# Row normalisation in a fused three-pass attention kernel: the subtract-and-scale step moved from VectorE to ScalarE, and every engine's order laid out anew

## The chip, the cores and the metric

The kernel runs on one core of a Trainium2 chip. The metric is the device time of one launch in microseconds. Engines are named as in the profile: PE (TensorE; PEld is its weight load), DVE (VectorE), ACT (ScalarE), POOL (GpSimd), SP (SyncE, here only an issuer of DMAs).

## The reference

A batch of 32 elements (`x`: 256 rows of 256, `ctx`: 120 rows of 256) goes through four transformer-like layers. Cut to what matters:

```python
def _ln(x, g, b):                       # in every layer, after every residual sum
    mu = mean(x, -1); var = mean((x - mu)**2, -1)
    return (x - mu) * rsqrt(var + EPS) * g + b
# L0: x += attn(ln(x)) causal, 16 heads; x += xattn(ln(x), ctx); x += gelu(ln(x) @ W_fc) @ W_mproj
# L1: x = ln(x + attn(x) masked); x = ln(x + xattn(x, ctx)); x = ln(x + relu(x @ W1) @ W2)
# L2: x = ln(x + xattn(x, ctx) masked)
# L3: x = ln(x + xattn(x, ctx) with 16 heads of 64)
```

All is float32, each layer has its own weights, and the softmaxes subtract the row maximum.

## The kernel before

The program makes three **passes** over the 32 elements: `l0` is layer L0, `l1` layer L1, `l2` layers L2 and L3 together. Between passes an element's rows go through DRAM (`between`). Within a pass an element is cut into **steps** with names such as `stats.1.0` or `scores_max.own.3`: `own` and `other` are the first and second attention, `ff` the feed-forward part, `three` the attention of L3, and 0 to 3 number the places where rows are normalised or turned.

**The order is written out by hand.** `LISTS[pass][engine]` gives every step a time in units of one element's period; `Step` adds `START[pass]` and the element's number, and `run` sorts each engine's steps by that sum (L367 and on). So each engine works on about six elements at once, always in the same cyclic order. An engine never looks past its next instruction: if that one waits on a semaphore, all behind it wait. The numbers decide the order only; nothing waits for a clock. The eight PSUM banks are handed out in the order of PE's list, each to the bank whose reader is listed to finish first, so a PE group can also wait for the DVE or ACT step that empties its bank.

**One normalisation** (key `0` to `3`) runs over these steps, each tile holding 2 x 128 rows:

- DVE `stats`: two `bn_stats`, two `bn_aggr` (L1023 to L1031) give `meanvar`.
- POOL `stats`: `veps` = variance + eps (L633), `rstd` = `veps` to the power -0.5 (L639).
- DVE `norm`: two `tensor_scalar`, one for each 128 rows, `xh` = (x - mean) * rstd (L1043, the loop of `kind == "norm"`).
- PE `norm`: four transposes of `xh` into a bank (L1328); ACT `norm`: gain and shift on the way out of the bank into `ht` and `ht_hi` (L757); POOL `ht_lo` where a product is split in parts.
- In `l1` and `l2` POOL `xb` makes `xh` * gain + shift as the next residual (L676, L681).

Normalisations 0, 1, 2 are made in `l0`, 1, 2, 3 in `l1`, 1 and 3 in `l2`: 8 for each element, 256 in all, of which 6 for each element feed PE; number 3 ends a pass and feeds only `xb` and the store.

**Around it.** Of an attention's `q` and `k`, three bfloat16 parts are made by ACT, DVE (`split_rest`, L1082), ACT and POOL, spilled to DRAM and loaded back stacked (`qstack`, `kstack`; SP, L558 and L572). `scores_max` is a first product on PE whose row maxima DVE takes (L1111, L1115); `scores_exp` the second, masked by DVE in `l1` (L1130) or on POOL in `l0` (L701), exponentiated by ACT (L879); `probs_v` the product with `v_aug`, which DVE writes (L1095); `project_out` ends it and DVE adds the residual into `xn` (L1210). SP loads `x_in` (L530) two elements ahead at most, after DVE's `project_out.own` of the element two before has read the buffer, and `ct` (L539) after PE's last `project_k3` of the element two before (in `l2`).

## Time and profile before

| what | value |
|---|---|
| median of 3 runs | 4299.66 us (4295.97 to 4301.73) |
| the profiled execution | 4300.15 us, its span 4298.4 us |
| PE busy, DVE busy | 4069.6 us (95%), 3742.6 us (87%) |
| ACT busy, POOL busy | 2718.3 us (63%), 1863.6 us (43%) |
| mean granted PE clock | 0.980 of full |
| DMA moved | 512.52 MB, 119 GB/s |
| PE idle in the span | 4298.4 - 4069.6 = 228.8 us |

Busy times overlap across engines. The passes have different loads, so the shares of the whole span are averages over three machines that differ; the rows below take them apart.

### The profile page before, as it was taken

Reading aid. Unit: us, or ns where it says so; the run is one execution under the profiler, and the core shown is the slowest. Engines: PE = TensorE matmul, PEld = TensorE weight load, DVE = VectorE, ACT = ScalarE, POOL = GpSimd, SP = SyncE. Lnnn points to the kernel's source line nnn. Section 1 sums busy time; section 2 is a strip of 40 time slices with the busy share of each in tenths; the row PEclk is TensorE's granted clock in tenths of the full one; section 3 lists DMA queues with packets and bytes.
Section 4 is the critical chain, followed back from the end, with each engine's and each line's share of the span. In section 5 each row is a group of like instructions: output and inputs, shape, how many; then the busy total and the mean of one; then the engine's idle time right before and its main releaser. Section 6 shows DMA issues by size and latency. Waiting matters only on the chain. (4 is left out here: it accounts for less than half of the span.)

```text
span 4298.4 us, 106109 instructions
## 1 busy us (share of the span) xinstructions
PE 4069.6 (95%) x36480; PEld 3458.8 (80%) x36480; DVE 3742.6 (87%) x12517; ACT 2718.3 (63%) x7085; POOL 1863.6 (43%) x3089
## 2 busy tenths in 40 slices
PE   4899999999999899999999999998999999999998
PEld 3688888888887678778778888777888888888887
DVE  4899999999998799999999999986888888888886
ACT  2566666667676555555555555554777777777776
POOL 4455545455554234445445455445222232222333
PEclk8999999999999899999999999999999999999999
DMA  4554545454554454544544544534223222222220
GB/s 149 151 153 142 156 142 161 137 155 140 149 152 117 127 169 117 147 138 119 146 139 125 158 125 133 152 109 119 81 61 84 69 75 75 70 82 71 75 72 27
DMA packets 403752, 512.52 MB, mean 119 GB/s; under 512 B 133648, under 2 KB 371216, under 8 KB 381712
## 3 DMA queue, kind: packets, MB, share of 16 engines
q1 hardware_dynamic: 395824, 495.51, 40.1%
q10 hardware_dynamic: 7392, 10.24, 0.7%
q8 instruction: 291, 4.77, 0.5%
q14 instruction: 245, 2.01, 0.2%
HBM read 266.30 MB, written 236.72 MB: 117 GB/s over the span
## 5 line engine op out<-in xcount | busy, mean ns | idle before, releaser
L879 ACT ACTIVATE probs_own<-bank 128x384 f32<-128x384 f32 (+2 forms) x1280 | 648.6, 564 | 286.1 <-DVE bank L1130 250.8
L633 POOL TENSOR_SCALAR veps<-meanvar 128x2 f32<-128x2 f32 x256 | 71.6, 280 | 1015.6 <-DVE meanvar L1031 1013.1
L1263 PE MATMUL bank<-w_ff,ffh 128*128 128x256 f32 x2048 | 490.1, 385 | 1.0
L1263 PE MATMUL bank<-kstack_own,qstack_own 96*128 96x256 bf16 (+2 forms) x3072 | 355.4, 250 | 102.9 <-issue 54.2
L1111 DVE CUSTOM_DVE_ANT_0 bank<-bank,mask_words 128x256 f32<-128x256 f32 x1024 | 398.3, 455 | 50.5 <-PE bank L1263 50.3
L1111 DVE DVE_READ_ACCUMULATOR2_ANT nmf_own<- 128x1 f32 x3072 | 429.1, 140 | 0.0
L1263 PEld LDWEIGHTS bank<-w_ff,ffh 128*128 128x128 f32 x2048 | 372.2, 190 | 65.5 <-issue 14.0
L879 ACT ACTIVATE probs_other<-bank 120x512 f32<-120x512 f32 x512 | 289.6, 603 | 161.3 <-PE bank L1263 161.1
L676 POOL TENSOR_TENSOR xb<-xh,vectors_l 128x256 f32<-128x256 f32 x320 | 229.8, 740 | 344.7 <-DMA out<-xb 202.8
L1263 PEld LDWEIGHTS bank<-kstack_own,qstack_own 96*128 96x128 bf16 x3072 | 242.7, 99 | 166.9 <-issue 95.3
L944 ACT ACTIVATE probs_other<-bank,negmax 128x120 f32<-128x120 f32 x1024 | 355.8, 380 | 31.0 <-DVE negmax L1229 31.0
L1111 DVE CUSTOM_DVE_ANT_0 bank<-bank,causal_rows 128x128 f32<-128x128 f32 (+1 forms) x1024 | 328.0, 391 | 23.0 <-PE bank L1263 22.7
L1263 PE MATMUL bank<-qstack_own,kstack_own 98*128 98x256 bf16 (+2 forms) x2560 | 320.8, 264 | 12.0 <-DMA qstack_own<-nm_t_own 9.2
L1130 DVE TENSOR_TENSOR bank<-bank,mask_words 128x512 f32<-128x512 f32 x512 | 319.1, 685 | 2.5 <-PE bank L1263 2.5
L1115 DVE TENSOR_REDUCE nmf_other<-bank 128x4 f32<-128x480 f32 x512 | 305.2, 646 | 14.7 <-PE bank L1263 14.6
L1263 PE MATMUL bank<-ht_hi,w_ff_hi 128*128 128x256 f32 x1024 | 314.2, 307 | 1.5 <-DVE nmf_own L1111 0.2
L1263 PE MATMUL bank<-probs_own,v_aug_own 128*32 128x256 f32 (+2 forms) x5120 | 299.6, 369 | 14.7 <-POOL probs_own L701 12.8
L1263 PE MATMUL bank<-ht_lo,w_ff_hi 128*128 128x256 f32 x1024 | 291.5, 285 | 0.0
L1263 PE MATMUL bank<-ht_hi,w_ff_lo 128*128 128x256 f32 x1024 | 291.0, 284 | 0.0
L1263 PEld LDWEIGHTS bank<-qstack_own,kstack_own 98*128 98x128 bf16 (+1 forms) x2560 | 231.7, 105 | 72.4 <-issue 15.0
L1111 DVE CUSTOM_DVE_ANT_0 bank<-bank,m_rows 128x120 f32<-128x120 f32 x1024 | 253.1, 316 | 28.5 <-PE bank L1263 28.5
L730 POOL TENSOR_TENSOR ht_lo<-ht,ht_hi 128x256 fp32r<-128x256 f32 x192 | 146.8, 786 | 245.0 <-ACT ht L757 245.0
(200 smaller groups left out, 12668.0 us busy)
## 6 DMA issues: line engine op xcount, KB each, us to landing
qstack_own<-q_parts SPq DMA_DIRECT2D x96, 768.0 KB, 5.7
kstack_own<-k_parts SPq DMA_DIRECT2D x64, 768.0 KB, 6.4
qstack_other<-q_parts SPq DMA_DIRECT2D x64, 768.0 KB, 6.1
q_parts<-q_parts_own SPq DMA_DIRECT2D x96, 384.0 KB, 3.5
k_parts<-k_parts_own SPq DMA_DIRECT2D x64, 384.0 KB, 2.5
q_parts<-q_parts_own SPq DMA_DIRECT2D x96, 256.0 KB, 3.0
q_parts<-other_parts SPq DMA_DIRECT2D x64, 384.0 KB, 3.0
other_words<-k_parts SPq DMA_DIRECT2D x64, 360.0 KB, 3.6
```

What stands on the lines that cost most here:

```text
L633: nc.gpsimd.tensor_scalar(veps[key][:, :], meanvar[key][:, :, 1], r["norms"][key]["eps"], None, ALU.add).then_inc(veps_ready.sem, 1)
L676: ins = nc.gpsimd.tensor_tensor(xb[key][:, t, :], xh[src][:, t, :], mul, ALU.mult)
L730: ins = nc.gpsimd.tensor_tensor(ht_lo[key][:, f, :], ht[key][:, f, :], ht_hi[key][:, f, :].bitcast(F32), ALU.subtract)
L879: nc.scalar.activation(probs[key][0:rows, j % a.slots, 0:n], bank_of(u)[0:rows, 0:n], ACT.Exp, scale=a.scale).then_inc(a_done.sem, 1)
L944: ins = nc.scalar.activation(probs3[:, j % 4, n, :], bank[:, n * S2:(n + 1) * S2], ACT.Exp, scale=-1.0, bias=negmax3[:, j, n:n + 1], accum ...
L1111: ins = v.tensor_tensor_reduce(scores, scores, add, -1.0, LIMIT if a.masked == "each" else 3.0e38, ALU.add, ALU.min, nmf[key][:, t, at:at ...
L1115: ins = v.tensor_reduce(nmf[key][:, t, first:first + FT * len(heads) - FT + 1:FT], bank[:, 0:len(heads) * nk].rearrange("p (h k) -> p h k" ...
L1130: v.tensor_tensor(p, p, add, ALU.add).then_inc(masked_by_dve.sem, 1)
L1263: return nc.tensor.matmul(out, lhsT, rhs, start=first, stop=True, skip_group_check=True)
```

## The change

The subtract-and-scale step leaves DVE. ACT makes `xh` as one `activation` of type Identity for each 128 rows, scale * x + shift, with a scale and a shift for each row: the scale is `rstd`, the shift is -mean * rstd. POOL makes the shift in two new instructions of 2 values for each partition: minus the mean (L640 in the new file), then times `rstd` (L649). The new step is named `xhat`; `xhat_ready` now counts ACT's steps, so everything that waited for DVE's `norm` (PE's transposes, POOL's `xb`, the writers of `xn`) waits for ACT. DVE's `bn_aggr` gets one more wait (`minus_ready`), and two mask steps of `l2` get waits on steps of their own engine. All numbers in `LISTS` and `START` are new.

```diff
-    xhat_ready = counts("xhat_ready", "DVE", ("norm",))
+    xhat_ready = counts("xhat_ready", "ACT", ("xhat",))
...
                 nc.gpsimd.tensor_scalar(veps[key][:, :], meanvar[key][:, :, 1], r["norms"][key]["eps"], None,
                                         ALU.add).then_inc(veps_ready.sem, 1)
...
+                nc.gpsimd.tensor_scalar(shift_of[key][:, :], meanvar[key][:, :, 0], -1.0, None, ALU.mult).then_inc(minus_ready.sem, 1)
...
-                nc.gpsimd.tensor_tensor(rstd[key][:, :], veps[key][:, :], half[:, :], ALU.pow).then_inc(rstd_ready.sem, 1)
+                nc.gpsimd.tensor_tensor(rstd[key][:, :], veps[key][:, :], half[:, :], ALU.pow).then_inc(pow_ready.sem, 1)
+                if w.new(minus_ready, u.tag):
+                    g.wait_ge(minus_ready.sem, w.value(minus_ready, u.tag))
+                settle(g)
+                if w.new(pow_ready, u.tag):
+                    g.wait_ge(pow_ready.sem, w.value(pow_ready, u.tag))
+                nc.gpsimd.tensor_tensor(shift_of[key][:, :], shift_of[key][:, :], rstd[key][:, :], ALU.mult).then_inc(rstd_ready.sem, 1)
...
+            elif kind == "xhat":
+                src = r["norms"][key]["src"]
+                x = x_in[:, u.element % 2] if src == "x_in" else xn[src]
+                if w.new(rstd_ready, ("stats", key, 0)):
+                    act_e.wait_ge(rstd_ready.sem, w.value(rstd_ready, ("stats", key, 0)))
...
+                for t in range(QT):
+                    ins = affine(xh[key][:, t, :], x[:, t, :], rstd[key][:, t:t + 1], shift_of[key][:, t:t + 1])
+                ins.then_inc(xhat_ready.sem, 1)
...
-                for t in range(QT):
-                    ins = v.tensor_scalar(xh[key][:, t, :], x[:, t, :], meanvar[key][:, t, 0:1], rstd[key][:, t:t + 1],
-                                          ALU.subtract, ALU.mult)
-                ins.then_inc(xhat_ready.sem, 1)
...
-START = {"l0": 0.00000, "l1": 32.78129, "l2": 66.17862}
+START = {"l0": 0.00000, "l1": 32.60944, "l2": 66.29325}
```

**Place 1, SP in `l1`,** up to the loads of `qstack_own` and `kstack_own` for the next element (L572 before, L575 with the change; `k_parts<-k_parts_own` is the spill of the third part of `k`, and in brackets stand the semaphores waited for). Before:

```order
L572 DMA other_words<-k_parts 96x1920 [waits a_full,spilled_k0_other,spilled_k1_other,spilled_k2_other]
L572 DMA qstack_other<-q_parts 96x4096 [waits spilled_q0_other,spilled_q1_other,spilled_q2_other]
L584 DMA between_2<-xb 128x2x256 [waits xb_ready]
L539 DMA ct<-in_ctx 128x2x120 [waits d_full]
L558 DMA k_parts<-k_parts_own 128x512
L530 DMA x_in<-between_1 128x2x256 [waits xb_ready,stored]
L572 DMA qstack_own<-q_parts 96x4096 [waits a_full,spilled_q0_own,spilled_q1_own,spilled_q2_own]
L572 DMA kstack_own<-k_parts 96x4096 [waits spilled_k0_own,spilled_k1_own,spilled_k2_own]
```

With the change:

```order
L533 DMA x_in<-between_1 128x2x256 [waits xb_ready,stored]
L575 DMA other_words<-k_parts 96x1920 [waits a_full,spilled_k0_other,spilled_k1_other,spilled_k2_other]
L561 DMA q_parts<-q_parts_own 128x512
L575 DMA qstack_other<-q_parts 96x4096 [waits spilled_q0_other,spilled_q1_other,spilled_q2_other]
L561 DMA k_parts<-k_parts_own 128x512 [waits lo_ready]
L575 DMA qstack_own<-q_parts 96x4096 [waits a_full,spilled_q0_own,spilled_q1_own,spilled_q2_own]
L575 DMA kstack_own<-k_parts 96x4096 [waits spilled_k0_own,spilled_k1_own,spilled_k2_own]
L587 DMA between_2<-xb 128x2x256
```

The store (`between_2<-xb`) and the load of `ct` stood ahead of the third spill of `k`; the store is now behind both stack loads and `ct` further up. From the row of negated maxima of `own` (`nm_rows.own`, L577), which waits for the end of `scores_max.own`, to that spill there were 13 other issues and are now 10.

**Place 2, PE in `l1`,** the end of the work that lies between the last `scores_exp.own` of one element (`qstack_own,kstack_own`, which frees both stacks) and the first `scores_max.own` of the next (`kstack_own,qstack_own`, which reads them anew). Ahead of these rows stood, after the last `scores_exp.own`, the 12 products of `project_q.other`. Before:

```order
L1263 MATMUL bank<-other_words,qstack_other 128x120 x16
L1263 MATMUL bank<-ct,w_other 128x120 x4
L1328 MATMUL bank<-ident,x_in 128x128 x4
L1263 MATMUL bank<-other_words,qstack_other 128x120 x8
L1263 MATMUL bank<-probs_own,v_aug_own 32x256 x8
L1328 MATMUL bank<-ident,xh 128x128 x4
L1263 MATMUL bank<-other_words,qstack_other 128x120 x8
L1263 MATMUL bank<-probs_own,v_aug_own 32x256 x8
L1263 MATMUL bank<-kstack_own,qstack_own 128x256 x8
L1263 MATMUL bank<-own_hi 128x256
```

With the change (ahead of these rows: 4 of `w_ff,ffh`, 20 of `other_words,qstack_other` and the same 12):

```order
L1288 MATMUL bank<-other_words,qstack_other 128x120 x8
L1353 MATMUL bank<-ident,x_in 128x128 x4
L1288 MATMUL bank<-ct,w_other 128x120 x4
L1353 MATMUL bank<-ident,xh 128x128 x4
L1288 MATMUL bank<-other_words,qstack_other 128x120 x4
L1288 MATMUL bank<-w_other,ct 120x256 x2
L1288 MATMUL bank<-kstack_own,qstack_own 128x256 x4
L1288 MATMUL bank<-probs_own,v_aug_own 32x256 x16
L1476 MATMUL bank<-identb,nm_parts_other 96x128 x2
```

The two groups of 8 `probs_own,v_aug_own` are moved behind the first `scores_max`; 4 `w_ff,ffh` and the 2 of `w_other,ct` are moved in. The trace counts each such float32 product twice (x8 for 4 rows here), and a product of `kstack`, `qstack` or `own_hi` once.

**Place 3, PE in `l2`,** ahead of the transposes of a freshly loaded `x_in`, which SP may load only after `project_out.own` (`w_own,ctx_t_own`) of the element two before and the DVE step behind it. With the change the whole stretch is:

```order
L1288 MATMUL bank<-w_own,ctx_t_own 128x256 x4
L1599 MATMUL bank<-ident,probs_other 120x128 x4
L1288 MATMUL bank<-kstack_own,qstack_own 128x120 x4
L1288 MATMUL bank<-w_own,ct 120x256 x2
L1288 MATMUL bank<-kstack_own,qstack_own 128x120 x4
L1288 MATMUL bank<-ct,ff_xu 128x120 x8
L1288 MATMUL bank<-kstack_own,qstack_own 128x120 x8
L1288 MATMUL bank<-ct,ff_xu 128x120 x8
L1353 MATMUL bank<-ident,x_in 128x128 x4
```

Before, only this was left of a longer one, in which a mask product, 16 of `vectors,probs_other`, 8 transposes of `probs_other` and 36 of `w_fc` stood between `w_own,ctx_t_own` and the first row here (the third row is the same transposes of `x_in`):

```order
L1263 MATMUL bank<-w_fc_hi,ot_lo 128x256
L1263 MATMUL bank<-kstack_own,qstack_own 128x120 x12
L1263 MATMUL bank<-ct,ff_xu 128x120 x8
L1263 MATMUL bank<-w_own,ct 120x256 x2
L1263 MATMUL bank<-kstack_own,qstack_own 128x120 x4
L1328 MATMUL bank<-ident,x_in 128x128 x4
L1574 MATMUL bank<-ident,probs_other 120x128 x4
L1263 MATMUL bank<-kstack_own,qstack_own 128x120 x4
L1263 MATMUL bank<-ct,ff_xu 128x120 x8
```

## Rows read from the trace of the kernel before

**Rows 1.** Windows: columns us, then busy (xcount) of PE, PEld, DVE, ACT, POOL; clock; DMA
```profile
306.10:1270.30 964.20, 937.88 (x8653) 792.76 (x8653) 899.60 (x2994) 653.17 (x1520) 511.26 (x920) 1.00 0.51 148
1715.90:2672.50 956.60, 912.30 (x7899) 762.49 (x7898) 902.00 (x2817) 524.02 (x1094) 472.86 (x756) 0.98 0.47 136
3200.00:4100.00 900.00, 900.00 (x8423) 797.45 (x8422) 747.77 (x2777) 677.00 (x2240) 261.53 (x409) 1.00 0.26 73
```

**Rows 2.** Source L1043, l0 and l1: ns min/median/max, first and last start
```profile
L1043 DVE TENSOR_SCALAR xh<-x_in,meanvar,rstd x48: 397/405/412, 306.1 to 1270.3; 128x256 f32<-128x256 f32 x48
...
L1043 DVE TENSOR_SCALAR xh<-xn_own,meanvar,rstd x44: 403/407/410, 1715.9 to 2672.5; 128x256 f32<-128x256 f32 x44
```

**Rows 3.** Waits of PE in those stretches (us, times, longest): l0, then l1
```profile
PE bank L1263 <- DMA qstack_own<-q_parts: 19.3, 22, 1.7
...
PE bank L1263 <- issue: 39.9, 21, 3.5
```

**Rows 4.** Timeline of PE in l1: start, us, what
```profile
1972.98 1.03 PE L1263 MATMUL bank<-kstack_own,qstack_own 96*128 96x256 bf16 x8 [1.89 <-issue]
...
2000.73 1.89 PE L1263 MATMUL bank<-w_ff,ffh 128*128 128x256 f32 x8
...
2007.47 1.03 PE L1263 MATMUL bank<-w_other,ct 128*120 128x256 f32 x4
...
2008.34 0.38 PE L1263 MATMUL bank<-qstack_own,kstack_own 98*128 98x256 bf16 x2
...
2014.75 1.07 PE L1263 MATMUL bank<-probs_own,v_aug_own 128*32 128x256 f32 x16
...
2018.06 1.03 PE L1263 MATMUL bank<-kstack_own,qstack_own 96*128 96x256 bf16 x8 [2.24 <-issue]
```

**Rows 5.** Timeline of SP's DMA issues in l1
```profile
1959.02 0.53 SPq L558 DMA_DIRECT2D k_parts<-k_parts_own  x1
...
1965.20 0.32 SPq L572 DMA_DIRECT2D kstack_own<-k_parts  x1
...
2009.03 0.32 SPq L572 DMA_DIRECT2D qstack_own<-q_parts  x1
```

**Rows 6.** Source L558, the spill issued at 1959.02
```profile
DMA to landing us min/median/max: 6.1/6.1/6.1
```

**Rows 7.** Source L572, the load issued at 1965.20
```profile
DMA to landing us min/median/max: 7.7/7.7/7.7
```

**Rows 8.** Timeline of DVE in l1
```profile
1972.32 0.71 DVE L1095 TENSOR_TENSOR v_aug_own<-bank,vectors_l 128x256 f32<-128x256 f32 x2
```

**Rows 9.** Lines, DVE, the stretch of l1: busy us, mean ns
```profile
L1043 DVE TENSOR_SCALAR xh<-xn_ff,meanvar,rstd 128x256 f32<-128x256 f32 x42 | 21.2, 547 | 0.1
...
L1043 DVE TENSOR_SCALAR xh<-xn_own,meanvar,rstd 128x256 f32<-128x256 f32 x43 | 15.8, 407 | 0.0
...
L1043 DVE TENSOR_SCALAR xh<-xn_other,meanvar,rstd 128x256 f32<-128x256 f32 x42 | 15.3, 405 | 0.0
```

**Rows 10.** Lines, ACT, the stretch of l1
```profile
L757 ACT ACTIVATE ht<-bank,columns_l 128x256 f32<-128x256 f32 x84 | 42.8, 563 | 19.1 <-PE bank L1328 19.1
```

**Rows 11.** Lines, POOL, the stretch of l0
```profile
L639 POOL TENSOR_TENSOR rstd<-veps,half 128x2 f32<-128x2 f32 x69 | 59.6, 864 | 10.9 <-POOL veps L633 10.4 <-DVE ot_raw_own L1165 0.4
...
L633 POOL TENSOR_SCALAR veps<-meanvar 128x2 f32<-128x2 f32 x69 | 21.4, 310 | 158.2 <-DVE meanvar L1031 158.2
```

**Rows 12.** Timeline of PE in l2
```profile
3505.80 2.00 PE L1263 MATMUL bank<-ct,ff_xu 128*128 128x120 f32 x16
...
3533.47 1.89 PE L1263 MATMUL bank<-w_own,ctx_t_own 128*128 128x256 f32 x8
```

**Rows 13.** Timeline of SP in l2
```profile
3536.60 0.38 SPq L530 DMA_DIRECT2D x_in<-between  x1
```

**Rows 14.** Source L530, loads of x_in in l2
```profile
DMA to landing us min/median/max: 2.6/2.7/4.8
```

More of the change, by code:

```diff
@@ new lines @@
+            scores_exp.own.9/1.95966 scores_exp.own.14/1.96311 scores_exp.own.12/1.96721 probs_v.own.2/2.01105
+            probs_v.own.3/2.02801 project_out.own.0/2.14529 norm.1.0/2.33009 project_q.other.0/2.39363 project_v.other.0/2.69626
+            scores_max.other.0/2.81664 scores_max.other.5/2.82192 scores_max.other.3/2.87023 scores_max.other.4/2.88377
+            scores_max.other.2/2.88906 scores_max.other.7/2.89434 scores_max.other.1/2.90378 scores_max.other.6/2.95438
+            negate_t.other.0/3.12816 scores_exp.other.7/3.24469 scores_exp.other.5/3.25017 scores_exp.other.1/3.25566
@@ new lines @@
+            scores_exp.own.4/2.04528 scores_exp.own.12/2.09166 scores_exp.own.11/2.09686 scores_exp.own.8/2.10205
+            scores_exp.own.14/2.10725 probs_v.own.0/2.11476 probs_v.own.1/2.13594 scores_exp.own.13/2.15942
+            scores_exp.own.9/2.20585 scores_exp.own.15/2.21105 project_k.other.0/2.33823 probs_v.own.2/2.40926
+            probs_v.own.3/2.43044 project_out.own.0/2.60333 norm.1.0/2.79363 project_q.other.0/2.83751 scores_max.other.5/3.25742
+            scores_max.other.1/3.26243 scores_max.other.2/3.26744 scores_max.other.3/3.27244 scores_max.other.4/3.27745
@@ L195 @@
+            spill_q.other.1/2.95410 spill_q.other.2/2.98879 stack_k.other.0/3.01121 stack_q.other.0/3.05317
+            nm_rows.other.0/3.48139 store.x.0/7.24343
         """,
@@ L445, in run @@
     veps_ready = counts("veps_ready", "POOL", ("stats",))
+    minus_ready = counts("minus_ready", "POOL", ("stats",))
+    pow_ready = counts("pow_ready", "POOL", ("stats",))
     rstd_ready = counts("rstd_ready", "POOL", ("stats",))
@@ L1056, in _ @@
                         dve.wait_ge(d_full.sem, w.value(d_full, tag, 1))
+                else:
+                    tag = latest(w, d_done, "scores_max", "own", len(r["atts"]["own"].max_jobs()), 1)
+                    if u.element % NB and w.new(d_done, tag, 1):
+                        settle(dve)
+                        dve.wait_ge(d_done.sem, w.value(d_done, tag, 1))
                 v.tensor_scalar(m_rows[:, :, :], m_in[:, :, :], 0.0, -BIG, ALU.not_equal, ALU.mult).then_inc(mask_ready.sem, 1)
@@ L1064, in _ @@
                         dve.wait_ge(a_full.sem, w.value(a_full, tag, 1))
+                else:
+                    tag = latest(w, masked_by_dve, "mask_scores", "own", r["atts"]["own"].exp_count(), 1)
+                    if u.element % NB and w.new(masked_by_dve, tag, 1):
+                        settle(dve)
+                        dve.wait_ge(masked_by_dve.sem, w.value(masked_by_dve, tag, 1))
                 rows = bank_of(u)[0:S2, 0:T // 2].bitcast(BF16)
```

354 lines of the change are left out of this document (173 added, 181 removed).

## The prediction

> **What bounds the kernel now.** I first cut the trace into one steady stretch for each pass [rows 1]; the reader should look at PE's busy time against the stretch, then at DVE's, then at the clock. The first starts of a repeated instruction give the period of an element [rows 2]: 24 pairs of `x_in` in `l0` are 23 periods, (1270.3 - 306.1) / 23 = 41.9 us, and 22 pairs of `xn_own` in `l1` are 21, (2672.5 - 1715.9) / 21 = 45.55 us. For one element that makes:
>
> - `l0`: PE busy 937.88 / 23 = 40.8 us, idle 1.1; DVE 39.1 us (93%).
> - `l1`: PE busy 912.30 / 21 = 43.4 us, idle 2.1; DVE 42.95 us (94%); clock 0.98.
> - `l2`: PE busy the whole 900 us; DVE 83%, ACT 75%. PE is the bound, nothing of another engine shows.
>
> So what can be won by moving work between the other engines lies in `l0` and `l1`. The clock of 0.98 in `l1` means 4% of the time at 1.2 instead of 2.4 GHz, which is 0.02 x 45.55 = 0.9 us of work lost for each element; in `l0` and `l2` it is 1.00. PE's own floor in `l1` is thus 43.4 - 0.9 = 42.5 us.
>
> Next I asked what PE waits for. In `l0` it is `qstack_own`, 19.3 / 23 = 0.84 us for each element; in `l1` 39.9 / 21 = 1.90 us, put down to "issue", so to nothing the view could name [rows 3]. With DVE at 94% one would guess DVE. The rows say otherwise: the gap ends at the first `scores_max.own` [rows 4], which waits for a bank and for the two stacks. The third part of `k` was spilled at 1959.02, landed 6.1 later, at 1965.1; `kstack_own` was issued at 1965.20 and landed 7.7 later, at 1972.9 [rows 5 to 7]. PE went on at 1972.98 [rows 4], while DVE was still writing `v_aug_own` until 1973.03 [rows 8]. **The gap of `l1` is the DMA chain spill, stack, product, not DVE**; DVE's idle 2.6 us are mostly PE's gap passed on.
>
> Two things hold that chain back. The spill is issued late, at the end of a burst of SP's issues. And the stacks can't be loaded before the last `scores_exp.own` of the element before has read them: it starts at 2008.34, `qstack_own` is issued at 2009.03, PE's other work lasts until 2014.75 + 1.07 = 2015.8, and the product starts at 2018.06 [rows 4, 5].
>
> **What the change removes from DVE.** In `l1` 21.2 + 15.8 + 15.3 = 52.3 us over 21 elements, 2.5 us each [rows 9]; DVE goes from 42.95 to 40.5 us. In `l0` it is as much or a little more, in `l2` two thirds. Since DVE isn't what PE waits for, this alone is worth nothing at once; it is room. Without it a gapless `l1` of 43 us would hold DVE at 100%, with it at 93%, a share that `l0` has now [rows 1].
>
> **What ACT gets.** Two instructions with a scale and a shift for each row. The nearest row is L757, the same kind with the same operands, from a bank: 0.563 us [rows 10]; a pair is 1.13 us at most, 3.4 us for an element with three. ACT was busy 653.17 / 23 = 28.4 us in `l0`, 25.0 us in `l1` [rows 1], so it ends at 31.8 of 42 and 28.4 of 45. In `l2`, 75% of 41.4 us (31.1) grows by 2.3 to 81%. I cost this at nothing; what hides it is that idle time, and if ACT's queue is late at that place, it comes out as the second rival.
>
> **What POOL gets.** Minus the mean is L633's kind, 0.31 us; the product with `rstd` is not in the trace: between L633's 0.31 and L639's 0.86, which is a power of the same two values [rows 11]. I take 0.4, nearer the former, for it has no power. Together 0.7 us, 2.1 for an element, on an engine busy 22.2 of 41.9 us in `l0`: nothing. As latency it counts: the chain from statistics to `xh` grows by 0.7 us on POOL (0.6 to 1.2) and by 1.13 - 0.8 = 0.3 us on ACT, so 1.0 us (0.9 to 1.5). It shows bare where no other element's work covers it: at the first element and at the last row sum of the program, 2 us in all. The new waits (`minus_ready`, the two mask steps) name work that was issued long before on engines which are in order anyway: nothing.
>
> **What the new orders do, `l1`.** Place 1: between the row of maxima and the third spill of `k` there are three issues fewer (the store among them, which also no longer moves its bytes beside the spill). An issue takes 0.3 to 0.5 us [rows 5], with the gaps between them about 0.5, so the spill goes out some 1.5 us earlier. Place 2: PE's cover was 7.5 us (2008.34 to 2015.8). The two groups of `probs_own` leave it (1.0 us each, of 1.07 with the tail), four `w_ff` (1.75, of 1.89) and the two `w_other,ct` (0.87, from 2007.47 to 2008.34) come in [rows 4]: 8.1 us. The stacks need, from the last `scores_exp.own`, 0.7 to the issue of `qstack_own`, 0.4 for the next issue, about 7.5 to land, 0.1 to start: 8.7 us. So the gap can't fall under 0.6 us and is 0.8 if the spill is a little late still, against 1.90: **1.1 us**. The clock fell in the gaps; at less than half their length I count a third of its 0.9 us as won back: **0.3 us**. Some 31 elements of `l1`: 31 x 1.4 = 43 us. The bounds: nothing (both are eaten by a longer landing), and 31 x 2.8 = 87 us.
>
> **`l0`.** The wait there is the same chain for `q`. Its rows around the stacks hardly move, except that the store now goes out just ahead of `qstack_own` instead of just behind. I take nothing; the bounds are 31 x 0.84 = 26 us gained and, for one issue of 0.4 us more, 12 lost.
>
> **`l2`.** PE is full, so nothing is to be won, but place 3 takes cover from the load of `x_in`. Before, the load was issued 3536.60 - 3533.47 = 3.1 us after `project_out.own` began and landed after 2.7 (at most 4.8) [rows 12 to 14]: it needs 5.8 us, at worst 7.9. The new stretch has 1.75 for `project_out`, twice 1.85 for `ct,ff_xu` (2.00 with the tail) [rows 12], 0.87 for `w_own,ct`, and 1.3 for 20 short products: 7.6 us. It holds by 1.8 us; at the worst landing it would be 0.3 us late. I take nothing; the bound is 31 x 0.3 = 9 us lost.
>
> **Sum.** -43 + 0 + 0 + 2 = -41 us. The profiled execution took 4300.15 us, so 4259 us; the median of the runs, 4299.66, is 0.5 us lower, which changes nothing.
>
> **The rivals.**
>
> *The gaps close fully.* If the spill is early and the stacks land fast beside less traffic, `l1` gives 31 x 2.8 = 87 and `l0` 20: 4300 - 107 + 2 = 4195 us. For it: DVE now has the room. Against: cover of 8.1 us for 8.7.
>
> *The normalisation chain comes onto PE's path (slower).* In none of the stretches did PE's transposes wait for `xh`; what it waited for is the row of each stretch shown [rows 3]. The chain grows by 1.0 us, and six normalisations for each element of the three passes feed PE: 192 chains. From 0.21 us shown of each, the 41 us are gone; with 0.4 us it is 77 - 41 = 36 us slower: 4336 us. For it: ACT serves `xh` in order among exponentials, which themselves wait for DVE's masks. Against: the orders were laid out with the longer chain in them.
> The length of POOL's instructions speaks for it too: `rstd` of 256 values in all takes 0.86 us on average in `l0` and 0.31 `veps` [rows 11], more than such small work asks. The Trainium skill's page "SBUF — State Buffer", section "Who interferes with whom", says that VectorE instructions with two inputs in SBUF and GpSimd's reads lock each other out for a whole instruction. By that rule each of the now four small instructions can be held up by such a DVE step, where it was two; the chain would grow by up to twice a DVE step more, and the rival gets likelier.
>
> *The moved work only changes the place of the wait.* A new order finds another late step, in `l0` and `l1`, and gives back what place 1 and 2 bring: 4298 us. If only the longer cover of place 2 holds (0.6 us for each of 31 elements), it is 4300 - 19 + 2 = 4283 us.
>
> **How the numbers follow.** Forecast 0.50; gaps closed 0.15; only place 2, 0.07; wait moved, no change, 0.09; chain on PE's path or another loss 0.19. A measurement here tells 0.2% (8.6 us) from no change. Faster by more: 0.50 + 0.15 + 0.07, less 0.02 for their weak ends, 0.70; same 0.09 and 0.01 of these, 0.10; slower 0.19 and 0.01, 0.20. The likeliest time is 4259 us. The range goes from the closed gaps (4195, and 5 us for the rest) to the price of the chain at 0.4 us: 4190 to 4336 us.
>
> **What would show it.** Right: in `l1` PE's longest wait drops under 1 us for each element, the period to about 44.2 us, the clock to 0.99, `kstack_own` issued within 0.5 us of `qstack_own`; DVE's busy time in `l1` near 40.5 us for each element; ACT's `xh` at 0.5 to 0.6 us; `l2` still full. Wrong: waits of PE for ACT's `xh` or for a bank read by DVE, PE idle in `l2`, or a spill of `k` that still lands 6 us before its stack is issued late.

## The result and the profile after

| | before | after |
|---|---|---|
| median of 4 runs, us | 4299.64 (4295.97 to 4301.73) | 4236.94 (4230.44 to 4241.72) |
| ratio | 1 | 0.9858, 95% interval 0.9846 to 0.987 |
| span of the profiled execution, us | 4298.4 | 4228.7 |
| PE busy, DVE busy, us | 4069.6, 3742.6 | 4036.3, 3593.2 |
| ACT busy, POOL busy, us | 2718.3, 1863.6 | 2976.9, 1990.4 |
| mean granted PE clock | 0.980 | 0.988 |

The time fell by 62.7 us; 41 were forecast. The two profiled spans, which the rows below take apart, differ by 69.7 us, for the profiled execution of after is the fastest of its four (4230.44 us). The sum is near, its parts are not.

I cut the spans at SP's loads of `x_in`, one for each element and pass: the 17th and 32nd lie in the steady part of `l0`, the 43rd and 64th in that of `l1`, the 73rd and 96th in that of `l2`. SP timeline of after, columns start and us:

```profile
646.86 0.38 SPq L533 DMA_DIRECT2D x_in<-in_x  x1
...
1263.03 0.38 SPq L533 DMA_DIRECT2D x_in<-in_x  x1
...
1777.25 1.73 SPq L533 DMA_DIRECT2D x_in<-between  x1
...
2691.21 0.36 SPq L533 DMA_DIRECT2D x_in<-between  x1
...
3131.12 0.38 SPq L533 DMA_DIRECT2D x_in<-between  x1
...
4095.15 0.38 SPq L533 DMA_DIRECT2D x_in<-between  x1
```

Each distance by its count of elements is a period: (1263.03 - 646.86) / 15 = 41.08 us. With the same loads of before (660.13, 1287.97, 1823.01, 2778.31, 3205.00 and 4157.37):

| stretch | before, us | after, us | difference |
|---|---|---|---|
| start to load 17 | 660.1 | 646.9 | -13.3 |
| loads 17 to 32: period of `l0` | 41.86 | 41.08 | -11.7 in all |
| loads 32 to 43, `l0` into `l1` | 535.0 | 514.2 | -20.8 |
| loads 43 to 64: period of `l1` | 45.49 | 43.52 | -41.3 in all |
| loads 64 to 73, `l1` into `l2` | 426.7 | 439.9 | +13.2 |
| loads 73 to 96: period of `l2` | 41.41 | 41.91 | +11.7 in all |
| load 96 to the end | 141.0 | 133.5 | -7.5 |

So up to load 32 (`l0`) 25 us were won, on the way to the 64th (mostly `l1`) 62, then 25 were lost in the turn to `l2` and in `l2`, and 7 came back at the end. In the turn from `l0` to `l1` (loads 32 to 43) the clock was 0.952 and is 0.977, and PE's busy time fell from 490.5 to 471.6 us; by 0.048 x 535.0 - 0.023 x 514.2, up to 14 of the 20.8 us can be the clock. The steady windows of after, same columns as [rows 1], in the order `l0`, `l1`, `l2`:

```profile
646.90:1263.00 616.10, 607.49 (x5642) 518.51 (x5640) 569.97 (x1861) 473.70 (x1080) 350.90 (x691) 1.00 0.53 151
1777.20:2691.20 914.00, 887.45 (x7898) 745.05 (x7897) 846.70 (x2689) 598.67 (x1219) 491.25 (x884) 1.00 0.50 143
3131.12:4095.15 964.03, 964.03 (x8926) 847.21 (x8925) 773.81 (x2832) 747.95 (x2462) 327.25 (x530) 1.00 0.26 73
```

The same loads 43 to 64 of before:

```profile
1823.00:2778.30 955.30, 910.38 (x7904) 760.83 (x7896) 901.56 (x2815) 523.75 (x1092) 472.87 (x756) 0.99 0.47 136
```

For one element, `l1` before (the same 21 elements): PE busy 43.35, idle 2.14 us; after: 887.45 / 21 = 42.26 busy, 1.26 idle, DVE 846.70 / 21 = 40.3 us. PE in `l2` is as full as it was, and yet an element takes 0.50 us longer with the same number of products (8926 against 8928 over 23 elements). What is left of [rows 3] in `l1` is one wait at the same place:

```profile
PE bank L1288 <- issue: 26.5, 21, 1.7
```

PE and SP around it, to be laid beside [rows 4, 5], and the landings of the two loads, beside [rows 6, 7]:

```profile
1960.03 0.60 PE L1288 MATMUL bank<-qstack_own,kstack_own 98*128 98x256 bf16 x4
...
1967.14 1.08 PE L1288 MATMUL bank<-w_other,ct 128*120 128x256 f32 x4
...
1969.20 0.60 PE L1288 MATMUL bank<-kstack_own,qstack_own 96*128 96x256 bf16 x4 [0.97 <-issue]
```

```profile
1956.02 0.36 SPq L561 DMA_DIRECT2D k_parts<-k_parts_own  x1
...
1960.95 0.32 SPq L575 DMA_DIRECT2D qstack_own<-q_parts  x1
...
1961.52 0.32 SPq L575 DMA_DIRECT2D kstack_own<-k_parts  x1
```

```profile
DMA to landing us min/median/max: 5.3/5.3/5.3
...
DMA to landing us min/median/max: 7.6/7.6/7.6
```

The third part of `k` is spilled 5.5 us before `kstack_own` is issued and lands at 1961.3, `kstack_own` goes out 0.57 us behind `qstack_own` (0.91 before), lands 7.6 us later, at 1969.1, and PE starts at 1969.20. The chain stands as the prediction described it. From the last `scores_exp.own` (1960.03) PE has work until 1968.2; the product starts 9.2 us after it.

In `l0` PE's wait for `qstack_own`, which the prediction took as staying, nearly went. Before and after, over 15 elements:

```profile
PE bank L1263 <- DMA qstack_own<-q_parts: 11.8, 14, 1.4
...
PE bank L1288 <- DMA qstack_own<-q_parts: 2.4, 6, 0.5
```

### The profile page after: what moved, and what is told of

Same layout as the page of the kernel before. It is cut to its first block and busy times, and to the rows that moved or that the text cites. A ratio compares the mean times of both kernels' runs of the same rounds, so it can differ in the third digit from the quotient of the medians.

```text
span 4228.7 us, 106986 instructions
## 1 busy us (share of the span) xinstructions
PE 4036.3 (95%) x36480; PEld 3441.3 (81%) x36480; DVE 3593.2 (85%) x12005; ACT 2976.9 (70%) x7597; POOL 1990.4 (47%) x3601
## 5 line engine op out<-in xcount | busy, mean ns | idle before, releaser
L905 ACT ACTIVATE probs_own<-bank 128x384 f32<-128x384 f32 (+2 forms) x1280 | 674.5, 563 | 173.2 <-PE bank L1288 106.1
L1288 PE MATMUL bank<-kstack_own,qstack_own 96*128 96x256 bf16 (+2 forms) x3072 | 384.7, 247 | 66.3 <-issue 40.3
L1288 PE MATMUL bank<-qstack_own,kstack_own 98*128 98x256 bf16 (+2 forms) x2560 | 339.5, 263 | 7.0 <-DMA qstack_own<-nm_t_own 2.9
L1136 DVE CUSTOM_DVE_ANT_0 bank<-bank,causal_rows 128x256 f32<-128x256 f32 (+1 forms) x1024 | 330.0, 392 | 18.5 <-PE bank L1288 17.0
L723 POOL TENSOR_TENSOR other_parts<-remains_other,other_parts 128x120 bf16<-128x120 f32 (+1 forms) x256 | 147.2, 596 | 385.5 <-issue 377.2
L1288 PE MATMUL bank<-probs_own,v_aug_own 128*32 128x256 f32 (+2 forms) x5120 | 287.8, 365 | 9.2 <-POOL probs_own L711 8.0
```

What stands on the lines that cost most here:

```text
L723: ins = nc.gpsimd.tensor_tensor(f3[2][:, f, :], x32[:, f, :], f3[1][:, f, :], ALU.subtract)
L905: nc.scalar.activation(probs[key][0:rows, j % a.slots, 0:n], bank_of(u)[0:rows, 0:n], ACT.Exp, scale=a.scale).then_inc(a_done.sem, 1)
L1136: ins = v.tensor_tensor_reduce(scores, scores, add, -1.0, LIMIT if a.masked == "each" else 3.0e38, ALU.add, ALU.min, nmf[key][:, t, at:at ...
L1288: return nc.tensor.matmul(out, lhsT, rhs, start=first, stop=True, skip_group_check=True)
```

## The experiments

Line numbers in rows of an experiment are those of its own file. Everything measured, the kernels before and after on top; the ratio is to runs of before made beside each kernel (their medians lie between 4297.20 and 4303.49 us), and the periods are read from the same loads of `x_in` in one execution each. Where a kernel has the tables and the code of before in a pass, its period there shows what one reading is worth: 41.86 to 42.03 us in `l0`, 45.49 and 45.23 in `l1`, 41.41 in all for `l2`. A difference under 0.3 us in `l1` or 0.2 in `l0` is therefore not told.

| kernel | median, us | ratio to before (95%) | `l0` | `l1` | `l2` |
|---|---|---|---|---|---|
| before | 4299.64 | | 41.86 | 45.49 | 41.41 |
| after | 4236.94 | 0.9846 to 0.9870 | 41.08 | 43.52 | 41.91 |
| op_only | 4314.93 | 1.0019 to 1.0042 | 42.52 | 45.07 | 41.41 |
| order_only | 4303.55 | 0.9998 to 1.0016 | 42.33 | 44.43 | 41.89 |
| dve_load | 4271.77 | 0.9925 to 0.9950 | 41.52 | 43.97 | 41.90 |
| sp_l1 | 4284.98 | 0.9943 to 0.9968 | 41.96 | 44.76 | 41.41 |
| pe_l1 | 4248.62 | 0.9862 to 0.9889 | 41.96 | 43.71 | 41.41 |
| both_moves | 4247.95 | 0.9857 to 0.9890 | 41.98 | 43.39 | 41.41 |
| cover_l1 | 4232.89 | 0.9824 to 0.9851 | 41.00 | 43.43 | 41.94 |
| best_b | 4223.99 | 0.9799 to 0.9830 | 41.10 | 43.34 | 41.41 |
| l2_old | 4231.53 | 0.9825 to 0.9852 | 41.11 | 43.57 | 41.41 |
| cover_l2_old | 4223.16 | 0.9803 to 0.9830 | 41.10 | 43.40 | 41.41 |
| split_l2 | 4330.82 | 1.0055 to 1.0081 | 42.03 | 45.23 | 42.17 |
| best_a | 4238.26 | 0.9849 to 0.9879 | 41.05 | 43.41 | 41.63 |

### The operation alone, and the order alone

```diff
 op_only: tables of before, code of after
-   "DVE": ... norm.1.0/2.29221 ...
+   "ACT": ... xhat.1.0/2.29221 ...
 order_only: tables of after, code of before
-   "ACT": ... xhat.1.0/2.29018 ...
+   "DVE": ... norm.1.0/2.29018 ...
```

One of eight such steps is shown for each. order_only keeps the two waits of the mask steps that the change added.

> The order tables and START of the kernel before; only xh is moved to ACT (each DVE norm step becomes an ACT step with the same number). Theory A (the gain is in PE's stretches and comes from the order: the DMA chain of l1 and what PE has ahead of it): PE still waits about 1.9 us for each element of l1, and the time stays within 9 us of before, 4291 to 4309 us. Theory B (DVE's relief of 2.5 us for each element is what pays): l1's period falls from 45.5 us towards 43.5 and l0's from 41.9 towards 41.1, so 4300 - 31 x 2.8 = 4213 to 4260 us. Theory C (the longer chain to xh comes onto PE's path, hidden in after by its order): slower than 4309 us.

> The order tables and START of the changed kernel, with xh still made by DVE (each ACT xhat step becomes a DVE norm step with the same number, POOL makes no shift). Theory A: l1's period 43.5 us, l0's 41.1, l2's 41.9 as in after; 4237 to 4250 us. Theory B: DVE at 87.6/22-like 42.8 us of 43.5 is too full, PE waits for banks that DVE reads, l1's period stays above 44.5 us: 4270 us or more.

Measured: 4314.93 and 4303.55 us. Neither half gives anything: the operation alone loses 14 us (against the 4300.76 us of before beside it), the order alone changes nothing that can be told, and together they win 63. PE's waits say why. op_only, `l1` over 21 elements, then `l0` over 15 (us, times, longest):

```profile
PE bank L1270 <- issue: 23.1, 21, 1.7
...
PE bank L1335 <- ACT ht L746: 17.4, 21, 0.9
...
PE bank L1270 <- DMA qstack_own<-q_parts: 17.6, 15, 1.7
...
PE bank L1270 <- DVE remains_own L1089: 10.0, 15, 1.0
```

In `l1` the gap of the DMA chain is smaller but there, and PE now waits 0.83 us for each element for ACT's `ht`, that is for an ACT queue made longer without being laid out for it (the reason is argued; that it is new is shown). `l1` is even so not longer than before (45.07 us, 0.42 less than that reading); what makes the kernel slower is `l0`, 0.66 us longer, where PE waits for the stack and for DVE. The wait for ACT is the second rival of the prediction, alive in the old order. order_only, `l1` and `l0`:

```profile
PE bank L1256 <- DVE nmf_other L1108: 16.9, 21, 1.4
...
PE bank L1321 <- DVE xh L1026: 9.2, 21, 0.4
...
PE bank L1256 <- DVE nmf_own L1104: 6.8, 15, 0.5
...
PE bank L1321 <- DVE xh L1026: 5.8, 14, 0.7
```

Of the DMA gap in `l1` 4.1 us are left (14 times, 0.6 at the longest), 0.9 in `l0`, and PE waits for DVE, for the row maxima and for `xh`: (16.9 + 9.2) / 21 = 1.24 us for each element of `l1`. Theory A as I had put it (the order does it all) falls, and so does B (the relief does it all), though B's account of this kernel, DVE too full for the new order, fits what PE waits for; C holds for op_only.

### Is it DVE's time, or `xh` that comes late?

```diff
 dve_load: after, with "norm" steps put back into DVE's tables at the numbers of ACT's xhat
+            elif kind == "norm":
+                ...
+                    for n in range(3):
+                        ins = v.bn_stats(junk[:, junks % 2 * 3 + n, :], ident[:, :])
```

> The changed kernel, with three small BN_STATS of a constant (128 x 128, their result is not used) put on DVE wherever order_only has DVE's norm step; xh stays on ACT. In order_only PE waited in l1 for DVE's nmf_other (16.9 us) and for DVE's xh (9.2 us) over 21 elements, in after for neither. Theory L (DVE's time at that place is what the new order needs free): l1's period rises from 43.5 towards 44.4 us, l0's from 41.1 towards 42.3, the wait for nmf_other is back, 4237 + up to 60 = 4270 to 4300 us. Theory M (not the load, but that xh itself comes late behind DVE's queue): the wait for nmf_other stays away, l1's period 43.5 to 43.8 us, 4237 to 4248 us.

Measured: 4271.77 us, 35 of the 63 us are lost again. PE's waits in `l1`, and the added work (41.4 us in 20.7 elements, 2.0 us each, against the 2.5 us that left DVE):

```profile
PE bank L1281 <- issue: 15.8, 21, 1.1
...
PE bank L1281 <- DVE nmf_own L1129: 5.5, 21, 0.5
...
PE bank L1281 <- DVE nmf_other L1133: 4.7, 21, 0.2
...
L1052 DVE BATCH_NORM_STATS2 junk<-ident 128x6 f32<-128x128 f32 x186 | 41.4, 278 | 0.0
```

The waits for the maxima are back, though not as long as in order_only, and the period rises by 0.45 us in `l1` and 0.44 in `l0`. So DVE's time counts in the new order (theory L), for about half of the difference to order_only in `l1` and a third in `l0`. Some of the rest may be load too, for DVE's busy time rises by only 1.7 us for each element of `l1` (40.3 to 42.0), in order_only by 2.4. The one wait of `l1` that order_only has and this kernel has not is the one for DVE's `xh`: there the transposes of `xh` start 45 ns behind DVE's semaphore in all 21 elements, 0.6 us later than their usual pace. That this wait makes up the rest is argued, not shown.

### The DMA chain of `l1`, on the kernel before

```diff
 sp_l1, table of SP in l1          pe_l1, table of PE in l1
-   spill_k.own.2/0.98890          -   project_q.own.0/0.33548
+   spill_k.own.2/0.93400          +   project_q.own.0/0.30500
-   store.x.0/6.96671
+   store.x.0/7.16550
```

> The kernel before with two steps of SP's table of l1 moved: the third spill of k goes right behind the second (about 2.2 us earlier, its data is there), the store behind kstack_own's load. In the trace of before, kstack_own is issued 0.9 us behind qstack_own (1965.20 against 1964.29) and lands 7.7 us later. Theory A1 (the late spill is half of l1's gap): kstack_own goes out 0.4 to 0.5 us behind qstack_own, the gap of 1.90 us shrinks by 0.5 (up to 0.9 if the store no longer slows the landing), and part of the 0.9 us of clock comes back: 31 x 0.7 = 22 us, 4278 us (4262 to 4285). Its rival (the spill is hidden behind the last scores_exp.own anyway and the landing stretches): 4300 us.

> The kernel before with one step of PE's table of l1 moved: project_q.own (12 products, 1.4 us) goes ahead of the first scores_max.own, so that PE has 1.4 us more to do while the stacks land. Theory A2 (PE's cover against the landing sets the gap): the gap falls from 1.90 to about 0.5 us, the clock rises from 0.98, l1's period from 45.5 to about 43.5 us; 31 x 1.9 = 59 us, 4241 us (4225 to 4260). Its rival (DVE at 94% holds l1: a bank isn't free, or scores_max is read later): the gap comes back at another place, 4290 us or more.

Measured: 4284.98 us, `l1` 0.73 us shorter (0.7 expected), and 4248.62 us, `l1` 1.78 us shorter (1.9 expected). PE's wait over 21 elements, of sp_l1 and of pe_l1, and the latter's window (columns as in [rows 1]):

```profile
PE bank L1246 <- issue: 33.7, 21, 2.2
```

```profile
PE bank L1246 <- issue: 10.0, 16, 2.0
...
1815.80:2733.70 917.90, 904.35 (x7908) 752.16 (x7903) 897.76 (x2815) 522.77 (x1092) 472.54 (x756) 1.00 0.49 142
```

Before it was 40.5 us in the same 21 elements; the clock of pe_l1 is 1.00. One step of PE moved by 0.03 of an element makes the time 1.25% shorter, some 54 us, with nothing else touched: the gap of `l1` was the DMA chain, and PE's cover is what it is measured against. DVE is busy 897.76 of 917.9 us here, 98%: a full DVE did not keep the gap open. Both together:

> The kernel before with the moves of sp_l1 and pe_l1 together, xh on DVE, l0 and l2 untouched. Alone they gave l1 periods of 44.76 and 43.71 us against 45.49. In pe_l1 DVE is busy 897.76 of 917.9 us, 42.75 us for each element. Theory V (with the gap closed DVE's 42.75 us hold l1, and that is what the move of xh to ACT takes away): l1's period falls by no more than 0.2 us to 43.5 to 43.7 us, 4240 to 4249 us. Its rival (the two add up: the DMA chain still sets l1): 43.71 - 0.73 = 42.98 us, DVE at 99%, 4249 - 22 = 4227 us.

Measured: 4247.95 us, `l1` 43.39 us. The window of both_moves:

```profile
1815.80:2720.00 904.20, 896.35 (x7856) 744.34 (x7855) 888.87 (x2802) 519.36 (x1086) 469.37 (x752) 1.00 0.51 142
```

DVE is at 98.3%, and PE itself at 99.1%. The second move brings 0.32 us where it had brought 0.73 alone, and in the median nothing that can be told from pe_l1: the two moves don't add up, as theory V has it, and `l1` stops at some 43.4 us. But PE's busy time is 43.0 us of them and DVE's 42.7, so this run does not show that it is DVE that stops it. That the moved `xh` opens room is shown by dve_load and order_only, in the new order.

### More cover in the changed kernel

```diff
 cover_l1: after, table of PE in l1        best_b: cover_l2_old, table of DVE in l1
-   probs_v.own.2/2.40926                  -   negate.other.1/3.43366
+   probs_v.own.2/2.39500                  +   negate.other.1/3.41500
-   probs_v.own.3/2.43044
+   probs_v.own.3/2.39600
```

> The changed kernel with two steps of PE's table of l1 moved: probs_v.own 2 and 3 (32 products, 1.87 us) go ahead of the first scores_max.own, which waits for kstack_own. PE's gap there is 1.27 us for each element. Theory A2: cover of 8.15 + 1.87 = 10.0 us against the 9.2 us that the stacks need from the last scores_exp.own: the gap closes, l1's period falls from 43.5 to 42.3 us, 31 x 1.25 = 39 us, 4198 us. Its rival (probs_own is not yet there so early, or DVE reads scores_max later and becomes the bound): the wait moves, 4230 us or more.

Measured: 4232.89 us, `l1` 43.43 us instead of 42.3; the interval overlaps that of after. The wait only moved, as the rival said. PE and DVE of cover_l1 in one element:

```profile
2018.85 0.60 PE L1270 MATMUL bank<-kstack_own,qstack_own 96*128 96x256 bf16 x4 [0.45 <-issue]
...
2020.33 0.28 PE L1458 MATMUL bank<-identb,nm_parts_other 128*96 128x128 bf16 x2 [0.88 <-DVE nm_parts_other L1151]
```

```profile
2016.91 0.17 DVE L1147 CAST nm_parts_other<-nmf_other 128x32 bf16<-128x32 f32 x1
...
2019.27 0.43 DVE L1118 CUSTOM_DVE_ANT_0 bank<-bank,mask_words 128x256 f32<-128x256 f32 x1 [2.18 <-PE bank L1270]
...
2020.00 0.18 DVE L1151 TENSOR_TENSOR nm_parts_other<-nmf_other,nm_parts_other 128x32 bf16<-128x32 f32 x1
```

PE's next wait is for `nm_parts_other`. DVE had nothing to do from 2017.1 to 2019.27, but that short step stands in its list behind a `scores_max.own` that waits for PE. So I moved it ahead:

> cover_l2_old with one further edit, in DVE's table of l1: negate.other.1 goes ahead of scores_max.own.8. In cover_l1 PE waits at negate_t.other 0.88 us for nm_parts_other, which DVE writes only behind the first scores_max.own, though DVE is idle for 2.2 us just before it. Theory Q (PE waits for what is queued behind a waiting step of DVE): the wait is gone, l1's period falls from 43.4 to 42.6 us (42.2 at best), 31 x 0.85 = 26 us, 4223 - 26 = 4197 us. Its rival (the stacks' load holds l1 at 43.4 us whatever else is moved): the time stays at 4223 us and the wait shows at the first scores_max.own.

Measured: 4223.99 us against 4223.16 of cover_l2_old, `l1` 43.34 us. The wait for `nm_parts_other` is gone (it does not appear in PE's waits any more) and nothing is won: PE waits for the next steps of DVE instead, in part in pieces that the view of waits counts as busy. PE of best_b around the place, and DVE:

```profile
2018.04 0.60 PE L1270 MATMUL bank<-kstack_own,qstack_own 96*128 96x256 bf16 x4
2018.92 0.36 PE L1270 MATMUL bank<-own_hi 128*128 128x256 f32 x1 [0.29 <-DVE nmf_own L1118]
...
2028.13 0.39 PE L1270 MATMUL bank<-ht_hi,w_ff_hi 128*128 128x256 f32 x1
```

```profile
2027.40 0.67 DVE L1217 TENSOR_TENSOR xn_own<-bank,xb 128x512 f32<-128x512 f32 x1
```

Four products of `scores_max.own` hold PE for 0.36 us when nothing stops them (timeline of cover_l1, 2020.45 to 2020.81); here they take 0.88 us, of which 0.29 are shown as a wait for DVE's row maxima (6.0 us in the 21 elements). The product at 2028.13 starts 0.06 us behind the end of DVE's `xn_own`, 0.39 us after the one ahead of it where 0.11 is the pace, and a third place loses 0.11 us behind `nmf_own`. The three make 0.9 us, what the wait for `nm_parts_other` was. From 2017.90 to 2028.8 the view shows no gap of DVE, so in this stretch PE follows DVE, though DVE is at 93% over the whole element. Whether a better order of that stretch would shorten `l1` was not tried.

### `l2`: a full PE whose period depends on the order

```diff
 l2_old: after, all tables of l2 from before (norm.k on DVE as xhat.k on ACT)
 cover_l2_old: l2_old and cover_l1 together
 split_l2: before, table of PE in l2
-   scores_max.own.5/1.16617 scores_max.own.3/1.32809 turn3.three.6/3.48900
+   scores_max.own.5/1.21600 scores_max.own.3/1.34400 turn3.three.6/3.49950
-   turn3.three.5/3.56846 scores_exp.own.0/1.61386 scores_exp.own.6/1.67545
+   turn3.three.5/3.61360 scores_exp.own.0/1.57750 scores_exp.own.6/1.70450
```

> The changed kernel with only the tables of l2 taken from before (DVE's norm steps as ACT's xhat steps at the same numbers). In both kernels PE is never idle in l2, yet its period is 41.41 us before and 41.91 after; PE goes 37 times for each element from one kind of product to another before, 43 times after. Theory S (each such change costs PE about 0.50 / 6 = 0.083 us): the period is 41.41 us again, 31 x 0.50 = 15 us are won, 4221 us. Theory X (the 0.50 us come with xh on ACT and the longer chain): the period stays at 41.9 us and the time at 4237 us.

> The kernel before with six steps of PE's table of l2 moved by 0.2 to 1.9 us each, so that PE goes 44 instead of 37 times for each element from one kind of product to another; nothing is added, and no other table changes. Theory S (a change costs 0.083 us): l2's period 41.41 + 7 x 0.083 = 41.99 us with PE still never idle, 31 x 0.58 = 18 us slower, 4318 us. Its rival (PE's time is the sum of its products in any order): 41.41 us, 4300 us. If PE shows idle time in l2, the moves made a wait and the run tells less.

> The changed kernel with the two moves of cover_l1 and the tables of l2 of before. If both theories hold and the two don't touch each other: 4237 - 39 - 15 = 4183 us. If l1's gap doesn't close by the moves: 4221 us.

Measured: l2_old has its period of 41.41 us again, with `xh` on ACT; order_only has 41.89 with `xh` on DVE, op_only 41.41 with `xh` on ACT. In all kernels the old tables of `l2` give 41.41 and the new ones 41.9 us, wherever `xh` is made; theory X is out. The time falls less than its 15 us, to 4231.53, and the interval overlaps that of after: the old tables take 142.6 us from load 96 to the end where the new ones take 133.5. split_l2 has 42.17 us, 0.76 more for 7 more changes of product, where 0.58 were expected. 0.06 of it are idle time of PE and 0.22 a wait that the busy share hides: the last `qstack_own,kstack_own` ahead of `w_v_hi,ct_parts` takes 0.33 us instead of 0.11 in all 23 elements, and the next product starts 44 ns behind the semaphore of ACT's `probs_other`. So 0.48 us are left for the 7 changes. l2_old together with cover_l1 is 4223.16 us, 14 us better than after: the two intervals don't meet. So far theory S held. Its test in the other direction:

```diff
 best_a: cover_l2_old, table of PE in l1 and in l2
-   negate_t.other.0/3.45392
+   negate_t.other.0/3.46500
-   scores_max.own.2/1.23870 scores_max.own.7/1.39392 scores_exp.own.5/1.67191 scores_exp.own.6/1.67545
+   scores_max.own.2/1.26350 scores_max.own.7/1.32900 scores_exp.own.5/1.63250 scores_exp.own.6/1.63300
-   scores3.three.2/2.80064 scores3.three.3/2.80064 turn3.three.3/3.07137
+   scores3.three.2/2.73150 scores3.three.3/2.73160 turn3.three.3/3.02450
```

> cover_l2_old with two further edits of PE's tables. In l1 negate_t.other, for which PE waited 18.6 us over 21 elements in cover_l1, goes 0.5 us later, behind two scores_max.own. In l2 seven steps are moved so that PE goes 31 instead of 37 times for each element from one kind of product to another. By theory S with 0.083 to 0.109 us for each change (l2_old and split_l2) l2's period falls from 41.41 to 40.76 to 40.91 us, 31 x 0.5 to 0.65 = 16 to 20 us; rival: the steps that are moved ahead wait for their data and the period stays. In l1 the wait of 0.9 us shrinks to 0.2 us: 31 x 0.7 = 22 us. Sum: 4223 - 18 - 22 = 4183 us; with neither 4223 us.

Measured: 4238.26 us; `l2` has 31 changes of product for each element and 41.63 us, more than the 41.41 with 37. (The edit in `l1` halved PE's wait there, from 18.6 to 9.4 us, and its period stayed at 43.41 us.) The window of `l2` over 23 elements still shows PE as never idle:

```profile
3127.50:4085.10 957.60, 957.60 (x8929) 840.38 (x8928) 771.45 (x2830) 755.28 (x2463) 295.96 (x529) 1.00 0.26 74
```

The rival that had been named is at work in it, unseen: one product of `probs_own,v_aug_own` and the last `qstack_own,kstack_own` ahead of `w_v_hi,ct_parts` take 0.13 and 0.12 us more than their pace in all 23 elements, and what follows each starts 44 ns behind a semaphore, of DVE's `ot_lo` and of ACT's `probs_own`. Without these waits it would be 41.38 us, and theory S wanted 40.76 to 40.91. **The price per change falls** all the same.

What does set it can be read one pair at a time, as the distance from one group's start to the next one's. The same eight products of `ct,w_own`, in before and in after:

```profile
3639.52 1.10 PE L1263 MATMUL bank<-ct,w_own 128*128 128x120 f32 x8
3640.39 0.36 PE L1263 MATMUL bank<-ht_hi,w_q_hi 128*128 128x256 f32 x1
3640.59 0.28 PE L1263 MATMUL bank<-ht_lo,w_q_hi 128*128 128x256 f32 x1
```

```profile
3558.44 1.10 PE L1288 MATMUL bank<-ct,w_own 128*128 128x120 f32 x8
3559.47 0.87 PE L1288 MATMUL bank<-ffh,other_parts 120*64 120x256 f32 x6
```

3640.39 - 3639.52 = 0.87 us when products of 128*128 weights follow, 3559.47 - 3558.44 = 1.03 us when those of 120*64 follow. About half of the 0.16 us is only counted at another product: in before the first `ht_hi,w_q_hi` has 0.20 us to the next one (3640.59 - 3640.39), where 0.12 is the pace. The other half is a price. The last `ct,w_own` of after takes 205 ns in all 23 elements, those inside the group 112; `ident,xh`, `ident,probs_other` and `qstack_own,kstack_own` take 201 to 203 ns instead of 108 or 109 where a group with weights of 64 rows or 64 columns follows, and keep their pace where others follow. An element of `l2` goes to or from weights of 64 rows or of 64 or 32 columns 9 times in before and 11 times in after; if the way back costs as much, which I can't tell apart, the two make 0.19 of the 0.50 us. split_l2 has 11 of them too and best_a 8, so this is a part and not the whole. Nor are the 0.50 us hidden waits: no product of `l2` in after starts late behind a semaphore as in best_a. Summed over 23 elements of each kernel, `ct,w_own` has 0.16, the transposes `ident,probs_other` 0.14, `ht,w_own` 0.13, the two split products 0.20, and the others give 0.1 back. The Trainium skill's page "TensorEngine Tiling (Array Packing)", section "Key Properties", says that changing the tiling mode drains TensorE; the trace agrees, by the 93 ns that the last product takes more.

## Why the prediction was right, and where it was not

**The bound of `l1`: right.** The chain of spill, stack and product closes the gap; sp_l1 and pe_l1 show it on the old kernel with three steps moved.

**Place 1 and 2: right in kind, the size off.** Forecast was a need of 8.7 us against a cover of 8.1, a gap of 0.8 us. The cover came out at 8.2 us (1968.22 - 1960.03), the need at 9.2 in the element shown, the gap at 1.26 us in the mean of 21: `kstack_own` waits 1.5 us for its issue after the last `scores_exp.own` began, where I had counted 1.1. Of the forecast 1.1 us, 0.67 came at this place (40.5 / 21 = 1.93 to 1.26), 0.88 in PE's whole idle time.

**The clock: the term right in size, and another one missing.** I counted a third of 0.9 us as won back, 0.3 us. Over loads 43 to 64 the clock was 0.986 before (0.99 in the row) and is 1.00, so no more than 0.014 x 45.49 = 0.6 us could come back, and both_moves, with the old operation at a clock of 1.00, has PE busy 43.02 us instead of 43.35: 0.3 us. But PE's busy time fell by 1.09 us in after. The other 0.76 us (43.02 to 42.26, both at 1.00) is a term that I did not have: the same products in another order. order_only shows that the two largest parts of it go with the order. There, as in after, `w_ff,ffh` takes 6.92 us of an element and `other_words,qstack_other` 1.68 and 1.67, from start to start; in before, op_only, pe_l1 and both_moves it is 7.12 and 1.88 us. (Its busy time as a whole is 42.84 us, for it holds hidden waits for `xh`.) Changes to or from weights of 64 or fewer rows or columns, as counted above for `l2`, are 8 in an element of `l1` before and 6 with the new order: what `l1` wins here `l2` pays. With all terms `l1` won 1.97 us for each element, where 1.4 was forecast: 31 of them make 61 instead of 43 us. Outside the steady `l1` I counted nothing for the clock; in the turn from `l0` (0.952 to 0.977) it can have given up to 14 us, where the term makes 9 in `l1`.

**"Since DVE isn't what PE waits for, this alone is worth nothing at once; it is room": right, and understated.** Alone it is worth less than nothing (op_only). But I gave the whole gain to the order and none to the room, and order_only shows that without it this order gives nothing: PE waits for DVE. The ratios of busy time that I named (DVE at 93% or at 100% of 43 us) were the right clue. I should have priced it as a condition of the `l1` term.

**"`l0`: I take nothing": wrong.** 0.78 us for each element, 25 us up to load 32, near the bound of 26 that I had set. I looked for what moved around the stacks, and nothing had; yet PE's wait for `qstack_own` fell from 0.79 to 0.16 us for each element, which is most of it. The gain is of the same kind as in `l1`: with either half alone `l0` is slower than before (42.52 and 42.33 us), with both it is faster. The operation alone leaves that wait (17.6 us in 15 elements), the order alone takes it away (0.9) and puts waits for DVE in its place (15.6). Which steps of the new order do it was not tried.

**"`l2`: PE is full, so nothing is to be won": true, but not that nothing can be lost.** The cover for the load of `x_in` held (no wait of PE in `l2`), and 0.50 us for each element were lost in a way I hadn't considered. The two misses, +25 in `l0` and -25 behind load 64, cancel by luck, and made the sum look better than its parts.

**ACT and POOL.** Estimated 0.563 us for each `xh`, measured (ns min/median/max), with the row of the estimate ahead of it:

```profile
L767 ACT ACTIVATE ht<-bank,columns_l x88: 556/563/569, 1707.0 to 2640.2; 128x256 f32<-128x256 f32 x88
...
L767 ACT ACTIVATE xh<-xn_other,shift_of,rstd x44: 585/594/604, 1703.2 to 2617.8; 128x256 f32<-128x256 f32 x44
```

ACT reads `xh`'s source from SBUF and the other's from a bank. The Trainium skill's page "ScalarE: Activation LUTs", section "What ACT_TABLE_LOAD costs", has 186 ns plus 93 for each of two pointer operands and 0.833 for each of 256 elements, which makes an estimate of 585 ns: the trace agrees, with 585 at the least and 594 in the median. POOL's two instructions, estimated at 0.7 us together, take 0.42 in `l1`:

```profile
L640 POOL TENSOR_SCALAR shift_of<-meanvar 128x2 f32<-128x2 f32 x66 | 14.7, 222 | 5.2
...
L649 POOL TENSOR_TENSOR shift_of<-shift_of,rstd 128x2 f32<-128x2 f32 x66 | 12.9, 195 | 5.2
```

Elsewhere the lock between DVE and POOL that spoke for the slower side is at work. Over all 256 the second has 194 ns at the least, 195 in the median and 646 at the most, with two over 200, so it is spared. But the first takes over 0.7 us instead of 0.22 in every other one of `l2`. One of them, with DVE at the same time:

```profile
3163.69 0.72 POOL L640 TENSOR_SCALAR shift_of<-meanvar 128x2 f32<-128x2 f32 x1
```

```profile
3163.69 0.64 DVE L1278 TENSOR_TENSOR probs_other<-probs_other,rec 128x480 f32<-128x480 f32 x1
```

In 29 such cases of the run POOL's instruction ends 81 to 86 ns behind that of DVE, which reads two tiles of SBUF. The Trainium skill's page "SBUF — State Buffer", section "Who interferes with whom", says that a VectorE instruction with two inputs in SBUF and a GpSimd instruction that reads SBUF shut each other out for the whole instruction; the trace agrees. It adds 0.5 us to half of the chains in `l2`, where PE is never idle, so it costs no time that can be seen. It had also lengthened the row that my estimate rests on: `veps` has 218 ns at the least in `l0` of before and 310 in the mean, `rstd` 708 and 868 (loads 17 to 32), each stretched in one of three.

The fill and drain, forecast 2 us longer, came out 7.5 us shorter at the end. That is the order: the new tables of `l2` store an element earlier (`store.x` at 5.42 instead of 6.54 periods), and the four kernels with the new code and the old tables of `l2` (op_only, l2_old, cover_l2_old, best_b) take 142.6 to 142.7 us from load 96 to the end. Against the 141.0 of before that is 1.6 us longer, in line with the forecast.

**The rivals.** In op_only it was ACT's queue (`ht`) that came onto PE's path, not `xh` itself; in after ACT's `xh` is behind 2.5 us of PE's waits in all 15 elements of `l0` together. The wait that moves (cover_l1, best_b) is what meets whoever goes on from here.

## What to carry to other kernels

Take work off an engine and lay the order out for it in one change: here the two halves gave -14 and nothing, and 63 us together, so a test of one half alone would have thrown both away. But before a new order of everything, try the one step that the timeline names: one group of PE moved ahead of the product that waits for its stack won 54 us, with the operation left where it was. Most of this change's gain could be had for one number. And judge a full engine by its period, not by its busy share: 41.41, 41.63, 41.91 and 42.17 us were all almost or wholly "busy", and in the second and the fourth waits of 0.25 and 0.28 us are in it.
